# Tokens' rows that carry gate and token to the experts, and expert tiles that return finished tokens

## The chip, the cores and the metric

The kernel runs on 1 core of one Trainium2 chip. The metric is the device time of one execution in microseconds (us), lower is better. All data is float32.

## The reference

Four blocks, each with a residual, over x of 8 x 256 tokens of width 128. Each block normalises its input first.

```python
x = x + attn_a(layernorm(x))      # 16 heads, relative bias, full 256 x 256 scores
x = x + ffn(layernorm(x))
x = x + attn_b(layernorm(x))      # 16 heads, low-rank keys and values, causal in blocks of T = 256
x = x + ffn(layernorm(x))

def ffn(x, ...):                  # 8 experts, each token goes to one
    logits = xt @ Wr + br
    gates = max(softmax(logits))
    idx = argmax(logits)
    xn = layernorm(xt) * ln_g + ln_b
    h = relu(xn @ W1[idx] + b1[idx])      # 128 -> 512
    y = h @ W2[idx] + b2[idx]             # 512 -> 128
    return y * gates
```

The gate of a token is one over the sum of exp(logit - largest logit).

## The kernel before

The program runs two stages, `st` 0 and 1, each an attention and then an expert part. The 2,048 tokens are 16 tiles of 128; two tiles are one batch entry `b` of 0 to 7. Every engine's program is one list over the same steps `s`: steps 0 to 63 of a stage are the attention's units (a batch entry and two heads), and from step 65 on (`n = s - 65`) one expert tile each. The order within a step is written out by hand (`step`, `after`, `routes`), so an engine does its instructions of a step in that order and waits in place for what is not there.

**Routing.** After a batch entry's attention, `post_a` and `post_a2` normalise it, GpSimd multiplies and adds ln_g and ln_b, `post_c` forms the logits and `choose` the one-hot choice on VectorE. TensorE counts (`post_d`), ScalarE copies the counts, and `place` on VectorE turns them into a row number in `xs_scratch` for each token. Entries 1, 3, 5, 6 and 7 route 4, 4, 4, 2 and 2 tiles. GpSimd sends a tile with one indirect DMA (`send`, L303): 128 rows of 129 floats, the normalised token and its own number. `xs_scratch`, one for each stage, is filled first with rows whose number is out of bounds (`fill`, L1454, SyncE's queue, 9 DMAs a stage).

**Experts.** A stage has 25 tiles of 128 rows. `index` computes where each tile's rows lie and which expert it has (part 3, at n = 11, for the last five). SyncE gathers tiles into `f_xs`, which has 24 slots (L1465). `XT` (L419) transposes them on TensorE in groups of four, ScalarE copies them out (L898), `H` (L668) multiplies by W1, ScalarE's `relu` (L906) follows, `Y` (L682) multiplies by W2. On VectorE `W` (L1309) copies the next tile's W1, b1 and b2, and `Y` (L1316) adds b2 to the result into one of 8 slots of `f_ys`. GpSimd's `back` (L322) scatters the slot to the tokens' rows of `ys_scratch`; rows with a number out of bounds are left out. Step n does H of tile n, Y of tile n - 2 and W of tile n + 2. TensorE's Y of a tile waits for VectorE's Y of the tile two before, and `W` waits for the `Y` that frees its buffer.

**Gates.** `gates` (L1332 and L930) forms them for 12 and then 4 tiles at n = 15 and n = 17: two VectorE instructions, Exp on ScalarE, two on VectorE.

**Return.** SyncE (`results`, L1478) reads `ys_scratch` into `xn`, in five pieces. VectorE's `add` (L1087) forms x + gate * y, in stage 0 before the next norm (`pre_a`, then GpSimd's power L291 and `pre_a2`), in stage 1 before the write to the output: the last piece is read by ScalarE's queue (L1016), added, and sent out by it (L1018).

## Time and profile before

| what | us |
|---|---|
| median of 3 runs | 693.21 |
| lowest and highest run | 689.38 and 693.81 |
| the profiled execution | 694.63 |
| its span, first to last instruction | 693.4 |
| around its span | 1.2 |

TensorE is busy for 94% of the span. The chain of waits follows the work that ended last back to the start; the timeline lists instructions in order of time; a bracket behind a row tells how long its engine had stood idle and what ended that. Windows give busy time per engine in a stretch. A queue's name (SPq, ACTq) marks the issue of a DMA.

### The profile page before, as it was taken

The page shows a single profiled execution, that of the slowest core. Times are in us where ns is not written, and L with a number is a line of the kernel's source. Part 1 is how long each engine was busy: PE and PEld are TensorE (multiplying, and loading weights), DVE is VectorE, ACT ScalarE, POOL GpSimd, SP SyncE. Part 2 cuts the span into 40 slices and gives each one's busy share as a digit, 9 for nine tenths or more (in the row PEclk, how much of TensorE's full clock was granted, in tenths as well). Part 3 has the DMA queues.
Part 4 walks back from the last instruction along what each step waited for, and adds up shares of the span by engine and source line. Part 5 has one row for each costly group of instructions (what it writes and reads, how often), then busy time and mean ns, then how long its engine had stood idle before and what let it go on. Part 6 is the DMA issues. An engine that isn't in the chain of part 4 may idle for free.

```text
span 693.4 us, 17716 instructions
## 1 busy us (share of the span) xinstructions
PE 655.1 (94%) x5406; PEld 551.3 (80%) x5406; DVE 471.9 (68%) x2113; ACT 534.2 (77%) x1768; POOL 361.1 (52%) x672
## 2 busy tenths in 40 slices
PE   6899999999999999999898999999999999989894
PEld 5678787888888888779796787888788888868893
DVE  3876767676777767966354668687768668896433
ACT  3788888788888879765664989898989889874462
POOL 3344635465556555636462446465745655644552
PEclk9999999999999999999998999999999999999998
DMA  9999999920000000014220000000000000020214
GB/s 265 193 182 180 211 248 182 183 38 6 1 6 5 9 1 10 24 40 151 79 63 16 2 1 3 1 1 6 14 2 1 10 10 1 17 47 17 78 31 127
DMA packets 71212, 42.71 MB, mean 62 GB/s; under 512 B 7953, under 2 KB 68254, under 8 KB 70864
## 3 DMA queue, kind: packets, MB, share of 16 engines
q1 hardware_dynamic: 66336, 36.31, 27.5%
q0 software_dynamic: 2624, 4.23, 1.9%
q10 hardware_dynamic: 2160, 1.05, 0.6%
q8 instruction: 45, 0.74, 0.5%
q14 instruction: 47, 0.39, 0.2%
HBM read 17.68 MB, written 25.06 MB: 62 GB/s over the span
## 4 chain that ended last, share of the span: by engine, by line
PE 79%; DVE 10%; issue 4%; ACT 3%; DMA 1%; POOL 1%; SPq 0%; DVEq 0%; POOLq 0%; ACTq 0%
PE ps L419 15%; PE ps L565 13%; PE ps L528 13%; PE ps L414 9%; PE ps L416 8%; PE ps L415 8%; PE ps L668 6%; PE ps L682 5%; DVE ring L1151 3%; ACT ring L857 1%; PE ps L602 1%; DMA wkn<-in_w_qkv 1%; ACT f_ht L906 1%; PE ps L620 1%; POOL ys_scratch L322 1%
## 5 line engine op out<-in xcount | busy, mean ns | idle before, releaser
L315 POOL TENSOR_SCALAR ring<-ring,rs 128x256 f32<-128x256 f32 (+1 forms) x500 | 220.0, 458 | 219.7 <-DVE rs L1162 218.7
L857 ACT ACTIVATE ring<-ring,mn 128x256 f32<-128x256 f32 (+1 forms) x512 | 243.4, 488 | 0.0
L419 PE MATMUL ps<-ident,ring 128*128 128x128 f32 x896 | 121.8, 275 | 3.7 <-POOL ring L315 2.4
L528 PE MATMUL ps<-qk 64*128 64x256 f32 (+1 forms) x1024 | 115.0, 363 | 0.2 <-ACT qk L825 0.2
L565 PE MATMUL ps<-pt,v 128*64 128x256 f32 (+1 forms) x1024 | 111.9, 359 | 2.0 <-DVE pt L1178 1.3
L419 PEld LDWEIGHTS ps<-ident,ring 128*128 128x128 f32 x896 | 102.2, 142 | 11.1 <-POOL ring L315 3.5
L857 ACT ACTIVATION_READ_ACCUMULATOR ring<-ring,mn 128x1 f32 x512 | 104.1, 203 | 0.0
L565 PEld LDWEIGHTS ps<-pt,v 128*64 128x64 f32 x1024 | 65.8, 136 | 46.2 <-issue 13.1
L528 PEld LDWEIGHTS ps<-qk 64*128 64x128 f32 x1024 | 82.6, 187 | 18.3 <-issue 8.5
L825 ACT COPY qk<-ps 128x512 f32<-128x512 f32 x128 | 74.8, 585 | 28.4 <-PE ps L416 26.9
L1151 DVE CUSTOM_DVE_ANT_0 ring<-ps,cm 128x128 f32<-128x128 f32 (+1 forms) x256 | 73.6, 350 | 6.3 <-PE ps L528 6.2
L322 POOL DMA_INDIRECT ys_scratch<-f_ys,f_xs x50 | 51.1, 1023 | 39.3 <-DVE f_ys L1316 27.3
L1180 DVE COPY pt<-ps 128x512 f32<-128x512 f32 x64 | 44.1, 689 | 35.2 <-PE ps L419 35.1
L414 PE MATMUL ps<-xth,wqkh 128*128 128x256 f32 x192 | 65.9, 343 | 0.0
L906 ACT ACTIVATE f_ht<-ps,f_w 128x128 f32<-128x128 f32 x136 | 38.5, 371 | 31.3 <-PE ps L668 25.3
L682 PE MATMUL ps<-w,f_ht 128*128 (+1 forms) x400 | 53.1, 278 | 5.6 <-DVE f_ys L1316 4.7
L1151 DVE CUSTOM_DVE_ANT_0 ring<-ps,T 128x256 f32<-128x256 f32 x136 | 55.4, 417 | 0.0
L416 PE MATMUL ps<-xtl,wqkh 128*128 128x256 f32 x192 | 55.0, 286 | 0.0
L415 PE MATMUL ps<-xth,wqkl 128*128 128x256 f32 x192 | 54.7, 285 | 0.0
L779 ACT ACTIVATE oh<-ps 128x512 fp32r<-128x512 f32 x64 | 38.4, 600 | 20.8 <-PE ps L565 20.8
L682 PEld LDWEIGHTS ps<-w,f_ht 128*128 128x128 f32 x400 | 48.2, 192 | 7.5 <-issue 7.3
L414 PEld LDWEIGHTS ps<-xth,wqkh 128*128 128x128 f32 x192 | 36.9, 192 | 18.7 <-issue 17.5
(209 smaller groups left out, 1339.2 us busy)
## 6 DMA issues: line engine op xcount, KB each, us to landing
xs_scratch<-padt SPq DMA_DIRECT2D x16, 1032.0 KB, 18.5
w<-in_W SPq DMA_DIRECT2D x16, 256.0 KB, 5.4
f_xs<-xs_scratch SPq DMA_DIRECT2D x50, 64.5 KB, 2.0
xs_scratch<-padt SPq DMA_DIRECT2D x2, 838.5 KB, 16.7
T<-in_bias SPq DMA_DIRECT2D x2, 512.0 KB, 8.2
T<-in_bias SPq DMA_DIRECT2D x1, 1024.0 KB, 11.1
bu<-in_w_kv_up SPq DMA_DIRECT2D x1, 1024.0 KB, 7.9
ys_scratch<-f_ys,f_xs POOLq DMA_INDIRECT x50
```

The costliest lines, as they stand in the source:

```text
L315: i = pool.tensor_scalar(ring[:, hh, it, 0:w], ring[:, hh, it, 0:w], rs[:, q], 1.0, ALU.mult, ALU.mult)
L322: pool.indirect_dma_start(ys_dram[st], bass.IndirectOffsetOnAxis(ap=f_xs[:, n % NX, 128:129].bitcast(U32), axis=0), f_ys[:, n % NY, :], No ...
L414: pe.matmul(out, ah, bh, start=first, stop=False)
L415: pe.matmul(out, al, bh, start=False, stop=False)
L416: return pe.matmul(out, ah, bl, start=False, stop=last)
L419: return pe.transpose(out, src, ident[:, :])
L528: i = pe.matmul(PS[u % 2][hh][:, 256 * it:256 * it + w], qk[rows, 128 * it:128 * it + 128], qk[rows, 256:256 + w], start=True, stop=True)
L565: i = pe.matmul(PO[64 * hh:64 * hh + 64, col + lo:col + 256], a_v[b % 2][:, jt, 128 * c + 64 * hh:128 * c + 64 * hh + 64], a_pt[(U0 + u) % ...
L682: i = pe.matmul(y_bank(n)[:, 0:128], f_ht[n % 3][:, 128 * f:128 * f + 128], w2[:, bass.ds(e * 4 + f, 1), :].rearrange("p a n -> p (a n)"), ...
L825: act.copy(a_qk[(U0 + u) % 2][:, :], PT_[:, :]).then_inc(a_t, 1)
L857: i = act.activation(ring[:, hh, it, 0:w], ring[:, hh, it, 0:w], ACT.Exp, bias=mn[:, q], scale=-1.0, accum_out=sm[:, q])
L1151: i = dve.tensor_tensor_reduce(ring[:, hh, it, 0:w], bank[:, 256 * it:256 * it + w], table(st, 2 * c + hh, it), 1.0, BIG, ALU.add, ALU.min ...
```

## The change

A token's row becomes `ROW` = 258 floats: normalised token (0 to 127), its number (128), its gate (129) and the token itself (130 to 257). `xn`, `numbers`, `gate` and `x` become views of one tile `row`. The fill, the sends and the gathers move 1,032 bytes a row. The slots of `f_xs` go from 24 to 12. The gates are formed route by route: one subtraction in `choose`, Exp on ScalarE one step later, the sum and the reciprocal in `place`. VectorE's `Y` has a second instruction that multiplies by the gate and adds the token. The scatter of stage 1 writes the output tensor; that of stage 0 writes `ys_scratch`, which is read back into `x`. `add`, `finish`, the final output DMAs and `d_out` and `v_end` are gone.

```diff
-NX = 24
+NX = 12
+ROW = 258
-POST = {"a": 14, "b": 15, "c": 16, "lg": 16, "d": 18, "place": 18}
-GATES = (15, 17)
+POST = {"a": 14, "b": 15, "c": 16, "lg": 16, "gate": 17, "d": 18, "place": 18}
...
-    xs_dram = [nc.dram_tensor(f"xs_scratch{st}", (XROWS, 129), F32).ap() for st in range(2)]
-    ys_dram = [nc.dram_tensor(f"ys_scratch{st}", (NT * 128, 128), F32).ap() for st in range(2)]
-    x = sb("x", [128, NT, 128])
+    xs_dram = [nc.dram_tensor(f"xs_scratch{st}", (XROWS, ROW), F32).ap() for st in range(2)]
+    ys_dram = [nc.dram_tensor("ys_scratch", (NT * 128, 128), F32).ap(), t["out"].rearrange("b s d -> (b s) d")]
+    row = sb("row", [128, NT, ROW])
+    xn, numbers, gate, x = row[:, :, 0:128], row[:, :, 128:129], row[:, :, 129:130], row[:, :, 130:ROW]
...
-    f_xs = sb("f_xs", [128, NX, 129])
+    f_xs = sb("f_xs", [128, NX, ROW])
...
-                xs_dram[st], bass.IndirectOffsetOnAxis(ap=posi[:, j:j + 1].bitcast(U32), axis=0), xn[:, j, :], None
+                xs_dram[st], bass.IndirectOffsetOnAxis(ap=posi[:, j:j + 1].bitcast(U32), axis=0), row[:, j, :], None
...
-        def gates(c):
-            m = CH[c][1] - CH[c][0]
-            act.wait_ge(v_gs, 2 * st + c + 1)
+        def gates(b):
+            r = NR * st + ROUTE_NO[b]
+            m = ROUTED[b][1] - ROUTED[b][0]
+            act.wait_ge(v_gs, r + 1)
             act.activation(f_sub[:, 0:m, :], f_sub[:, 0:m, :], ACT.Exp).then_inc(a_ge, 1)
...
+            if (b := post_at(s, "gate")) is not None and b in ROUTED:
+                gates(b)
             if (b := post_at(s, "d")) is not None and b in ROUTED:
                 post_d(b)
...
-        j0, j1 = BACK[-1]
-        for i in range(NY):
-            act.wait_ge(d_ys[i], 2 * 16 * len(range(i, NF, NY)))
-        act.dma_start(xn[:, j0:j1, 0:128], ysv[1][:, j0:j1, :]).then_inc(d_yt[-1], 16)
-        act.wait_ge(v_end, len(BACK))
-        act.dma_start(ov[:, j0:j1, :], x[:, j0:j1, :]).then_inc(d_out, 16)
...
         V(dve.tensor_reduce(g, l, AX, ALU.max))
+        dve.tensor_tensor(f_sub[:, 0:n, :], l, by_tile(g, n), ALU.subtract).then_inc(v_gs, 1)
         V(dve.tensor_tensor(h, l, by_tile(g, n), ALU.is_ge))
...
         V(dve.tensor_copy(bas[:, 0, :], run[:, :]))
+        dve.wait_ge(a_ge, r + 1)
+        G = gate[:, t0:t1, :].rearrange("p t a -> p (t a)")
+        V(dve.tensor_reduce(G, f_sub[:, 0:n, :], AX, ALU.add))
+        V(dve.reciprocal(G, G))
         dve.wait_ge(a_cnt, r + 1)
...
-                add(0, 2 * b)
-                V(add(0, 2 * b + 1))
+                for j in range(2 * b, 2 * b + 2):
+                    dve.wait_ge(d_yt[BACK_OF[j]], 16)
...
-            dve.tensor_tensor(f_ys[:, n % NY, :], y_bank(n)[:, 0:128], first_layer(n)[:, 512:640], ALU.add
-                              ).then_inc(v_fy, 1)
+            V(dve.tensor_tensor(f_ys[:, n % NY, :], y_bank(n)[:, 0:128], first_layer(n)[:, 512:640], ALU.add))
+            dve.scalar_tensor_tensor(f_ys[:, n % NY, :], f_ys[:, n % NY, :], f_xs[:, n % NX, 129:130], f_xs[:, n % NX, 130:ROW],
+                                     ALU.mult, ALU.add).then_inc(v_fy, 1)
...
-                sp.dma_start(xn[:, j0:j1, 0:128], ysv[st][:, j0:j1, :]).then_inc(d_yt[g], 16)
+                sp.dma_start(x[:, j0:j1, :], ysv[:, j0:j1, :]).then_inc(d_yt[g], 16)
...
-        results(1, 0)
-        results(1, 1)
-        for g, (j0, j1) in enumerate(BACK[:-1]):
-            sp.wait_ge(v_end, g + 1)
-            sp.dma_start(ov[:, j0:j1, :], x[:, j0:j1, :]).then_inc(d_out, 16)
-        sp.wait_ge(d_out, 16 * len(BACK))
+        for i in range(NY):
+            sp.wait_ge(d_ys[i], 2 * 16 * len(range(i, NF, NY)))
```

A gather of tile n of 12 or more waits, by the code that was there, until the scatter of tile n - NX has landed; with 24 slots only tile 24 did.

## Rows read from the trace of the kernel before

**Rows 1.** The page: busy time, share of the span and instructions of each engine

```profile
PE 655.1 (94%) x5406; PEld 551.3 (80%) x5406; DVE 471.9 (68%) x2113; ACT 534.2 (77%) x1768; POOL 361.1 (52%) x672
```

**Rows 2.** Chain of waits in order of time, its end: start, us, what

```profile
684.65 2.29 DMA ys_scratch<-f_ys,f_xs
686.94 0.02 issue
686.96 2.60 DMA xn<-ys_scratch
689.56 0.02 issue
689.58 1.14 DVE x L1087 x4
```

**Rows 3.** Timeline of the last 11 us: start, us, engine, line, idle before

```profile
683.59 0.29 DVE L1316 TENSOR_TENSOR f_ys<-ps,f_w 128x128 f32<-128x128 f32 x1 [1.30 <-PE ps L682]
683.79 3.23 DVE L1087 SCALAR_TENSOR_TENSOR x<-xn,gate,x 128x128 f32<-128x128 f32 x12
...
690.75 0.38 ACTq L1018 DMA_DIRECT2D out<-x  x1
```

**Rows 4.** Who waited for `f_ys`, us and times, over the whole span

```profile
  PE ps L682: 4.7, 4
  DVE f_w L1309: 1.7, 7
```

**Rows 5.** Windows: us; busy us (instructions) of PE, PEld, DVE, ACT, POOL; PEclk, DMA share, GB/s

```profile
78.00:92.00 14.00, 14.00 (x114) 11.42 (x112) 9.54 (x41) 12.33 (x38) 7.02 (x15) 1.00 1.10 351
...
95.00:130.00 35.00, 35.00 (x285) 28.85 (x282) 25.80 (x113) 29.17 (x91) 16.88 (x35) 1.00 1.27 182
...
150.00:180.00 30.00, 30.00 (x242) 24.58 (x239) 20.64 (x89) 24.30 (x73) 16.93 (x33) 1.00 0.02 6
```

**Rows 6.** Timeline, VectorE, stage 0, the last batch entry beside tiles 1 to 4

```profile
313.58 0.28 DVE L1188 TENSOR_TENSOR x<-ps,x 128x128 f32<-128x128 f32 x1
313.90 0.29 DVE L1189 TENSOR_TENSOR x<-ps,x 128x128 f32<-128x128 f32 x1
...
323.57 0.17 DVE L1073 TENSOR_TENSOR bas<-cnt,bas 128x8 f32<-128x8 f32 x1 [0.86 <-ACT cnt L880]
```

**Rows 7.** Instructions of `gate`: durations min/median/max in ns

```profile
L1087 DVE SCALAR_TENSOR_TENSOR x<-xn,gate,x x32: 321/346/465, 361.3 to 690.4; 128x128 f32<-128x128 f32 x32
```

**Rows 8.** Timeline, all engines, stage 1, tiles 8 to 11

```profile
653.23 0.29 DVE L1316 TENSOR_TENSOR f_ys<-ps,f_w 128x128 f32<-128x128 f32 x1 [3.67 <-PE ps L682]
653.32 1.14 ACT L906 ACTIVATE f_ht<-ps,f_w 128x128 f32<-128x128 f32 x4 [2.62 <-remote]
...
653.78 1.15 PE L682 MATMUL ps<-w,f_ht 128*128 x8 [1.61 <-DVE f_ys L1316]
...
656.22 1.15 PE L682 MATMUL ps<-w,f_ht 128*128 x8 [0.85 <-DVE f_ys L1316]
```

**Rows 9.** Waits, TensorE, 605 to 686 us: us in total, times, longest

```profile
PE ps L419 <- DMA f_xs<-xs_scratch: 0.4, 1, 0.4
...
PE ps L668 <- DVE f_w L1309: 0.3, 1, 0.3
```

**Rows 10.** Timeline around the hand-over to stage 1

```profile
361.33 0.61 DVE L1087 SCALAR_TENSOR_TENSOR x<-xn,gate,x 128x128 f32<-128x128 f32 x2
...
362.58 0.98 POOL L322 DMA_INDIRECT ys_scratch<-f_ys,f_xs  x1 [0.30 <-issue]
...
363.57 0.75 POOL L291 TENSOR_TENSOR rstd<-rstd,half 128x2 f32<-128x2 f32 x1
...
367.44 0.41 PE L414 MATMUL ps<-xth,wqkh 128*128 128x256 f32 x1
...
375.60 0.28 PE L414 MATMUL ps<-lth,wqkh 128*128 128x256 f32 x1
```

**Rows 11.** Timeline, SyncE's queue: the fills of both stages, the first gathers

```profile
21.07 42.30 SPq L1454 DMA_DIRECT2D xs_scratch<-padt  x9
...
86.88 46.56 SPq L1454 DMA_DIRECT2D xs_scratch<-padt  x9
291.25 8.71 SPq L1465 DMA_DIRECT2D f_xs<-xs_scratch  x12
```

**Rows 12.** Windows, columns as in rows 5: where the fill of stage 0 ends

```profile
72.00:74.00 2.00, 2.00 (x17) 1.83 (x17) 1.62 (x7) 1.74 (x4) 1.74 (x4) 1.00 0.72 94
74.00:76.00 2.00, 2.00 (x20) 1.79 (x20) 1.40 (x4) 2.00 (x8) 1.08 (x3) 1.00 0.37 15
```

**Rows 13.** Instructions of `xs_scratch`: ns min/median/max, first and last start in us

```profile
L303 POOL DMA_INDIRECT xs_scratch<-xn,posi x32: 957/1102/1261, 134.6 to 647.5; - x32
```

**Rows 14.** DMA issues: count, KB each, median us from issue to landing

```profile
f_xs<-xs_scratch SPq DMA_DIRECT2D x50, 64.5 KB, 2.0
```

**Rows 15.** Timeline, stage 1: scatter of tile 11, and the transposes of tiles 20 to 23

```profile
659.30 0.98 POOL L322 DMA_INDIRECT ys_scratch<-f_ys,f_xs  x1 [0.30 <-issue]
...
668.97 0.60 PE L419 MATMUL ps<-ident,f_xs 128*128 128x128 f32 x4
```

**Rows 16.** Windows, columns as in rows 5: the hand-over, and stage 1's tiles 8 to 17

```profile
366.00:376.00 10.00, 8.85 (x44) 7.03 (x45) 2.26 (x14) 2.73 (x5) 0.97 (x1) 0.66 0.10 28
...
650.00:672.00 22.00, 19.20 (x168) 18.59 (x167) 7.02 (x31) 13.04 (x44) 10.79 (x11) 1.00 0.25 69
```

More of the change, by code:

```diff
@@ L68 @@
 PRE_0 = {"a": -4, "a2": -3, "b": -2, "c": -1}
[L70 to L72 removed]
+LAST_POST = {"sums": 68, "a": 69, "b": 70, "c": 70, "lg": 71, "gate": 71, "d": 71, "place": 72}
+POST = {"a": 14, "b": 15, "c": 16, "lg": 16, "gate": 17, "d": 18, "place": 18}
 INDEX = {60: 0, 62: 1, 65: 2, 76: 3}
@@ L987, in step @@
                 next_weights(n)
-            if n in GATES:
-                gates(GATES.index(n))
         def after(s):
@@ L1083, in start_rows @@
         V(dve.tensor_copy(run[:, :], rows_e[:, 0:NE]))
-    def add(st, j):
-        dve.wait_ge(d_yt[BACK_OF[j]], 16 * (st + 1))
-        return dve.scalar_tensor_tensor(x[:, j, :], xn[:, j, 0:128], gate[:, j:j + 1], x[:, j, :], ALU.mult, ALU.add)
     def table(st, h, it):
@@ L1416, in step @@
                 next_weights(n)
-            if n in GATES:
-                gates(GATES.index(n))
-            if st and NF + 1 <= n < NF + 3:
-                for j in ((0, 1, 2, 3), range(4, 12))[n - NF - 1]:
-                    finish(j)
         def routes(s):
@@ L1445, in dve_program @@
                 steps[1](s - OFF)
-        for j in range(*CH[1]):
-            finish(j)
     def fill(st):
```

47 lines of the change are left out of this document (15 added, 32 removed).

## The prediction, made before the result was known

> **What bounds the kernel now.** I read the page first: TensorE is busy for 94% of the span, VectorE for 68%, ScalarE for 77%, GpSimd for 52% [rows 1]. So what counts is what TensorE waits for, and what stands behind its last matmul. Then the end of the chain of waits: the last scatter lands at 686.94, is read back for 2.60 us, four additions take 1.14 us, and the output DMA is issued at 690.75 [rows 2, 3]. The reader is to see that from 683.88 to 693.4 no matmul runs, and that all after 686.94 is the return of tokens. Then the waits for `f_ys` and the timeline of the expert parts, for where VectorE holds TensorE up: TensorE waits on it 4 times in both stages, and the weight copy 7 times [rows 4]. Last the windows, for what the fill costs: 285 matmuls in 35 us beside it and 242 in 30 us without it, 8.1 a us in both, TensorE busy throughout [rows 5]. The fill costs the attention nothing.
>
> **The end.** Removed is all between the last landing, 686.94, and the end of the span, 693.40, but for the 0.04 us in which a queue sees it (the chain shows 0.02 at each such step [rows 2]): 6.42 us. The scatter goes to the output with the same 512 bytes a row; nothing shows a write to another tensor to cost otherwise, so it lands as before. Also gone are 12 additions that lay beside the scatters [rows 3], worth nothing here.
>
> **VectorE's Y.** It now has a dependent second instruction. A dependent pair starts 0.32 us apart (313.58 and 313.90 [rows 6]); the removed addition has the very form of the new instruction and takes 0.346 us [rows 7]. A tile is thus done 0.32 + 0.346 = 0.67 us after its start where it was 0.29 [rows 3]: +0.38 us. 50 of them are 19 us of VectorE's time, nearly all beside matmuls. Where it is not hidden:
> - The last tile: the scatter behind it starts 0.38 later. +0.38.
> - Tiles 8 and 9 of each stage. TensorE's Y of tile 10 waited 1.61 us for VectorE's Y of tile 8; then the 11 small instructions of `index` part 3, then Y of tile 9, for which TensorE's Y of tile 11 waited 0.85 us [rows 8]. Both are in one chain: 2 x 0.38 = 0.76.
> - Seven weight copies waited for a Y [rows 4], and TensorE's H waited once for such a copy in stage 1 [rows 9]; I take one a stage: 0.38. But ScalarE stood 2.62 us and VectorE 3.67 us just before tile 8's Y, and the trace doesn't name the cause of the first ("remote") [rows 8]; a standstill of another cause would swallow what came before it. So 0.76 to 1.14 a stage; I take 1.0, for two stages +2.0. The bounds: 0, if other waits end last, and (4 + 7) x 0.38 = 4.2 for both stages, if each wait seen is lengthened in full.
>
> **The hand-over to stage 1.** Two additions before the norm go, 0.61 us [rows 10]. But the norm's power (L291) stands on GpSimd behind the scatter of tile 22, which ran until 363.56; the power started at once [rows 10]. That scatter waits for VectorE's Y, so it comes 0.38 later and the 0.61 is won where nobody waits. +0.38, between -0.3 and +0.4. In the attention of stage 1 fourteen more additions go, from an engine that has slack there: nothing.
>
> **The gates.** Route by route: three instructions of VectorE of about 0.17 us (the small ones of `place` [rows 6]) and a short Exp, five times a stage. The two in `place` stand before the wait for the counts. For the last entry that wait was 0.86 us [rows 6], which covers both; the one in `choose` delays the count by 0.1 to 0.2 us, and TensorE transposes a group before it counts. Behind `place` stand the W and Y of the next tiles, and GpSimd's two sends. In the attention VectorE is busy for 20.64 of 30 us and ScalarE for 24.30 [rows 5], and both orders leave a step between Exp and its reader. Cost 0, at most 0.2 a route. The eight old instructions at tiles 13 and 15 go; no TensorE wait stands there. 0.
>
> **The rows of 1,032 bytes.** The fill: its 9 DMAs are issued from 21.07 on [rows 11], and the traffic falls to 94 and then 15 GB/s between 72 and 76 [rows 12], so it ends near 75: 54 us. The bytes double. If each byte costs what it costs now, at 182 GB/s, it ends at 21 + 108 = 129; at the 351 GB/s at which the weights load in other pieces, at 75 [rows 5]. The first send, which waits for it, is at 134.6 [rows 13]. So it is hidden, with 5 us to spare at worst. The second fill, whose issue starts 23.5 us behind the end of the first's [rows 11], would at the lower rate end near 129 + 23 + 108 = 260; the first gathers stand behind it on SyncE's queue at 291 [rows 11].
> The sends: 1.10 us on GpSimd each [rows 13], for 128 rows. If that counts rows, nothing changes; if a wide row counts as two, each doubles. I take the first, since the row count alone stays.
> The gathers: 64.5 KB land in 2.0 us [rows 14]; the added 64.5 KB are 0.18 us at 351 GB/s and 0.35 at 182. TensorE waited 0.4 us for the first group in stage 1 [rows 9], so a delay there counts. I take 0.3 a stage, +0.6, between 0 and 4 x 0.35 x 2 = 2.8.
> The Trainium skill, DMA: Bandwidth & Descriptors, Anatomy of one DMA, has a DMA cost about 2 us fixed plus its bytes at 436 GB/s. By it the added half is 0.15 us and the term 0.3 instead of 0.6; the trace's 2.0 us for 64.5 KB agrees.
>
> **Twelve slots.** A gather of tile 23 now waits for the scatter of tile 11, which starts at 659.30 and, at 2.29 us like the last one [rows 2], lands at 661.6; the gather lands 2.0 later, at 663.6, while its transposes are at 668.97 [rows 15]. 5 us of cover; behind it on SyncE's queue stand only tile 24's gather and the read-back. The groups before have scatters long done. 0.
>
> **The sum**, against the profiled execution's span: -6.42 + 0.38 + 2.0 + 0.38 + 0.6 = -3.06, from 693.4 to 690.3 (691.6 with the 1.2 around it). The profiled execution is 1.4 above the median of the runs; the same difference from the median, 693.21, gives 690.2.
>
> **The rivals.**
> - *All the VectorE work is hidden.* For it: only 4 waits of TensorE on `f_ys` [rows 4], and a standstill of unnamed cause before the two I charge. Against: both waits stand with their lengths. -6.42 + 0.38 + 0.38 = -5.7: 687.5.
> - *It is hidden and the clock stays up.* The clock falls at the hand-over: the mean is 0.66 of full in the 10 us from 366 [rows 16], so 6.8 us at 1.2 GHz after TensorE had stood for parts of the 2 us before; a 128x256 matmul takes 0.41 us there and 0.28 at 2.4 GHz [rows 10]. If it didn't fall, 6.8 x (1 - 0.28 / 0.41) = 2.2 more are won: 685.3. Little speaks for it, the gap gets no shorter by my sum.
> - *The clock falls in the expert parts.* They run at 1.00 now [rows 16] with waits of 1.61 and 0.85 us close together [rows 8], which get longer. One such fall costs 2.2, as above, two stages 4.4: -3.06 + 4.4 = +1.3: 694.5. The Trainium skill, TensorE: Matmul & The Clock Gate, The HAM clock gate, says that idleness halves the clock; the trace agrees at the hand-over and does not show it at the waits of tiles 10 and 11.
> - *Wide rows count double on GpSimd.* Then the two last sends before tile 12's gather come 2 x 1.1 = 2.2 us later a stage, and TensorE waits for that group: 4.4, again 694.5. For it: nothing in the trace, whose rows of 512 and 516 bytes are too alike.
> - *The fill blocks the first send* (the slower side). GpSimd waits at L303 for the whole fill, and behind it stands the scaling of the softmax (L315), on which TensorE's transposes wait. It decides when the fill takes over 134.6 - 21.1 = 113.5 us, 2.1 times now for twice the bytes; each us beyond is a us of the kernel, and from 123.5 us (2.3 times) on the kernel is over 1% slower than before. At three times, 162 us: +48.5 - 3.1 = 45 slower, 739. For it: only 5 us to spare, and the present rate is half of that of the weights, so bytes aren't all that a fill costs. Against: the pieces get larger, and for the byte price to rise they would have to run worse than the small ones.
>
> **How the numbers follow.** About 1% (7 us) is what a measurement of this kernel can tell from no change. Chances: my forecast 0.50, hidden 0.17, hidden with the clock 0.08, clock falls 0.08, sends double 0.10, fill blocks 0.07. The likeliest gives 690.2. The range, 686.5 to 695.5, takes in the forecast, the hidden case, the clock's fall and the doubled sends, 0.85 together; the upper bounds of Y (+2.2) and of the gathers (+2.2) together lead to 694.6. Faster by over 1% needs under 686.3: the case with the clock, and little for the spread of runs, 0.10. Slower needs over 700.1: the fill in most of its cases, and two of the others together, 0.07. Within 1%: 0.83.
>
> **What would show it.** Right: the span ends within 0.1 us of the last scatter's landing; VectorE's Y pair takes 0.67 us; the waits of TensorE's Y of tiles 10 and 11 grow by about 0.4 each; the first send still starts near 134.6; the hand-over's power starts right behind a scatter. Wrong: sends over 1.5 us on GpSimd, a gather of tiles 12 to 23 ahead of its transposes by nothing, a granted clock under 1.00 between 630 and 670, or attention steps that got longer.

## The result, and the profile after

| what | before, us | after, us |
|---|---|---|
| median of 7 runs each | 692.03 | 686.75 |
| lowest and highest run | 689.38 and 693.81 | 685.44 and 688.04 |
| profiled execution | 694.63 | 687.1 |
| its span | 693.4 | 685.9 |

The ratio after to before is 0.992, 95% interval 0.990 to 0.9941: 5.3 us less, 0.8%. That is inside "within 1%", and inside the forecast range by only 0.25 us (its lower end is 686.5). But 3.1 us less was forecast, so the size has to be explained.

The page of after first, busy time by engine:

```profile
PE 652.9 (95%) x5406; PEld 549.8 (80%) x5406; DVE 482.1 (70%) x2145; ACT 533.3 (78%) x1774; POOL 358.8 (52%) x672
```

VectorE is busy 10.2 us longer than in [rows 1], TensorE 2.2 us less, with the same 5,406 matmuls. Where the time went is seen when each execution is cut at the same instructions: the start of ScalarE's copy of a unit's queries and keys (attention), of the first `relu` of a tile (expert part), and of the last scatter. These starts are read off the traces. The 48 units are units 8 to 55 of the 64 of an attention, in every run.

| stretch, us | before | after | difference |
|---|---|---|---|
| 48 units of stage 0's attention | 213.17 | 213.17 | 0.00 |
| stage 0, relu of tile 0 to tile 12 | 38.12 | 39.30 | +1.18 |
| stage 0, tile 12 to tile 24 | 24.12 | 23.57 | -0.55 |
| tile 24 to stage 1's first unit | 7.77 | 8.15 | +0.38 |
| 48 units of stage 1's attention | 188.21 | 186.29 | -1.92 |
| stage 1, tile 0 to tile 12 | 37.14 | 38.41 | +1.27 |
| stage 1, tile 12 to tile 24 | 22.80 | 23.00 | +0.20 |
| last relu to last scatter | 3.55 | 3.95 | +0.40 |
| last scatter to the end of the span | 8.74 | 2.11 | -6.63 |

The spans differ by 7.5 us. 1.6 of that lie ahead of unit 8 of stage 0; there the two profiles of before (before and before_again) differ by 2.1 from each other, so the change need have no part in it. The rest, 0.3, lies in the stretches between those of the table. The second profiles of both kernels, on other chips, give before 23.36 for stage 0's tiles 12 to 24 (so the -0.55 is spread), and the same 188.15 and 186.30 for stage 1's attention. For tile 24 to stage 1's first unit they give 7.37 and 7.63: this stretch differs by 0.4 to 0.5 between profiles of one kernel, and its 0.38 is read from one wait below instead.

**The end.** The timeline of after (start, length in us, engine, line, output<-input; in brackets the idle time before and what ended it):

```profile
682.29 0.29 DVE L1313 TENSOR_TENSOR f_ys<-ps,f_w 128x128 f32<-128x128 f32 x1 [0.91 <-PE ps L682]
682.61 0.35 DVE L1314 SCALAR_TENSOR_TENSOR f_ys<-f_ys,f_xs 128x128 f32<-128x128 f32 x1
683.76 0.98 POOL L322 DMA_INDIRECT out<-f_ys,f_xs  x1 [0.61 <-issue]
```

The reader is to see the pair of VectorE, whose second starts 0.32 us behind the first and takes 0.35, and that nothing follows the last scatter: it starts at 683.76 and the span ends at 685.9. In [rows 2, 3] a read of 2.60, four additions and an output DMA followed the same scatter.

**The weight copies.** Waits of TensorE in after, from 310 to 330 us (stage 0) and from 627 to 641 us (stage 1); us in total, times, longest:

```profile
PE ps L668 <- DVE f_w L1306: 0.7, 1, 0.7
PE ps L620 <- ACT pT L872: 0.5, 1, 0.5
```

Both windows give these two lines. Before, the first was 0.3 in both stages (for stage 1 see [rows 9]). It is H of tile 5, and VectorE in after shows why (timeline, stage 1):

```profile
633.15 0.28 DVE L1313 TENSOR_TENSOR f_ys<-ps,f_w 128x128 f32<-128x128 f32 x1
633.47 0.35 DVE L1314 SCALAR_TENSOR_TENSOR f_ys<-f_ys,f_xs 128x128 f32<-128x128 f32 x1
633.97 0.50 DVE L1306 COPY f_w<-w 128x644 f32 x1
```

```profile
634.52 1.16 PE L668 MATMUL ps<-f_xt,f_w 128*128 128x128 f32 x8 [0.67 <-DVE f_w L1306]
```

The new instruction stands ahead of the copy, which starts 0.82 us behind the start of Y (0.42 in before), and TensorE's H starts when the copy ends. Its wait is 0.67 and 0.67 us in the two stages of after, 0.28 and 0.28 in before, and the same to 0.01 in the second profiles. Relu of tile 4 to tile 5 is 2.33 us before and 2.72 after in both stages.

**Tiles 8 to 11.** Timeline of after, stage 1:

```profile
650.85 2.17 ACT L906 ACTIVATE f_ht<-ps,f_w 128x128 f32<-128x128 f32 x8 [3.29 <-PE ps L668]
650.95 0.29 DVE L1313 TENSOR_TENSOR f_ys<-ps,f_w 128x128 f32<-128x128 f32 x1 [1.69 <-remote]
...
652.14 1.15 PE L682 MATMUL ps<-w,f_ht 128*128 x8 [0.79 <-ACT f_ht L906]
...
654.72 1.15 PE L682 MATMUL ps<-w,f_ht 128*128 x8 [0.65 <-DVE f_ys L1314]
```

Where [rows 8] has waits of 1.61 and 0.85 for VectorE, after has 0.79 for ScalarE and 0.65 for VectorE. These two did not grow. But after has a third one just ahead, at H of tile 11, where before has none:

```profile
648.76 0.50 DVE L1306 COPY f_w<-w 128x644 f32 x1
649.31 1.16 PE L668 MATMUL ps<-f_xt,f_w 128*128 128x128 f32 x8 [1.09 <-issue]
```

The row names nobody who ended it; H starts 0.05 us behind the end of the weight copy. The three waits of tiles 10 and 11 make 2.53 us in stage 1 (2.46 in before) and 2.76 in stage 0 (2.25 in before). Beside them ScalarE and GpSimd stand still as well, as in before, and no cause is named for it ("remote").

**The hand-over.** Timeline of after:

```profile
360.91 0.29 DVE L1033 BATCH_NORM_STATS2 stats<-row 128x6 f32<-128x128 f32 x1
...
362.16 0.98 POOL L322 DMA_INDIRECT ys_scratch<-f_ys,f_xs  x1 [0.30 <-issue]
...
363.15 0.74 POOL L291 TENSOR_TENSOR rstd<-rstd,half 128x2 f32<-128x2 f32 x1
363.93 0.66 DVE L1044 TENSOR_SCALAR xh<-row,mv,rstd 128x128 f32<-128x128 f32 x2 [1.08 <-POOL rstd L291]
```

The power starts 0.01 us behind the scatter, as in [rows 10]; VectorE had its part ready at 361.88, 1.3 us earlier. TensorE's wait for the output of this norm, first in before and then in after:

```profile
365.16 0.41 PE L419 MATMUL ps<-ident,xh 128*128 128x128 f32 x2 [0.70 <-DVE xh L1049]
```

```profile
364.74 0.41 PE L419 MATMUL ps<-ident,xh 128*128 128x128 f32 x2 [1.08 <-DVE xh L1044]
```

It is 0.70 and 1.08 in the second profiles too: +0.38.

**The fill and the sends.** One window of after beside the second fill (columns as in [rows 5]), and the instructions of `xs_scratch` on GpSimd (ns min/median/max, first and last start):

```profile
95.00:130.00 35.00, 35.00 (x286) 28.61 (x286) 25.83 (x113) 29.52 (x93) 17.74 (x36) 1.00 1.10 314
```

```profile
L303 POOL DMA_INDIRECT xs_scratch<-row,posi x32: 959/1078/1253, 133.4 to 644.9; - x32
```

The same 35 us moved 182 GB/s at a DMA share of 1.27 before [rows 5] and 314 GB/s at 1.10 after. The sends take what they took [rows 13], and the first starts at 133.4. TensorE ran 286 matmuls beside it (285 before).

### The profile page after: what moved, and what is told of

It reads as the page before. It is cut to its first block, busy times and chain, and to the rows that moved or that the text cites. A ratio compares the mean times of both kernels' runs of the same rounds, so it can differ in the third digit from the quotient of the medians.

```text
span 685.9 us, 17753 instructions
## 1 busy us (share of the span) xinstructions
PE 652.9 (95%) x5406; PEld 549.8 (80%) x5406; DVE 482.1 (70%) x2145; ACT 533.3 (78%) x1774; POOL 358.8 (52%) x672
## 4 chain that ended last, share of the span: by engine, by line
PE 82%; DVE 9%; issue 3%; ACT 2%; POOL 1%; DMA 1%; another core or an unknown queue 1%; SPq 0%; DVEq 0%; POOLq 0%; ACTq 0%
PE ps L419 16%; PE ps L565 14%; PE ps L528 14%; PE ps L414 10%; PE ps L416 8%; PE ps L415 8%; PE ps L668 5%; PE ps L682 4%; DVE ring L1148 2%; DMA wvn<-in_w_qkv 1%; PE ps L602 1%; PE ps L620 1%; ACT f_ht L906 1%; DVE f_ys L1314 1%
## 5 line engine op out<-in xcount | busy, mean ns | idle before, releaser
L419 PE MATMUL ps<-ident,ring 128*128 128x128 f32 x896 | 120.4, 274 | 2.5 <-POOL ring L315 2.4
L419 PEld LDWEIGHTS ps<-ident,ring 128*128 128x128 f32 x896 | 102.4, 142 | 8.2 <-POOL ring L315 3.5
L1148 DVE CUSTOM_DVE_ANT_0 ring<-ps,T 128x256 f32<-128x256 f32 x136 | 55.5, 417 | 0.0
L1148 DVE CUSTOM_DVE_ANT_1 ring<-ps,T 128x256 f32<-128x256 f32 x120 | 50.0, 417 | 0.0
```

What stands on the lines that cost most here:

```text
L419: return pe.transpose(out, src, ident[:, :])
L1148: i = dve.tensor_tensor_reduce(ring[:, hh, it, 0:w], bank[:, 256 * it:256 * it + w], table(st, 2 * c + hh, it), 1.0, BIG, ALU.add, ALU.min ...
```

## The experiments

Names that begin with a are edits of after, with b edits of before. They ran in four series, each on another chip, with before in each. Ratios are to before, with their 95% interval; behind stand the median of the edit and that of before in its series. Four questions: what the end is worth and why; whether Y costs what was charged; which edit gives the 1.9 us in stage 1's attention; what wide rows and gates cost.

### The end

**a_tail_back**: after, but stage 1's scatters go to a second scratch tensor, and the tokens are read back and written out by two DMAs each way on SyncE, without additions.

```diff
-    ys_dram = [nc.dram_tensor("ys_scratch", (NT * 128, 128), F32).ap(), t["out"].rearrange("b s d -> (b s) d")]
+    ys_dram = [nc.dram_tensor(f"ys_scratch{st}", (NT * 128, 128), F32).ap() for st in range(2)]
...
+        sp.dma_start(x[:, j0:j1, :], ysv1[:, j0:j1, :]).then_inc(d_yt[-1], 16)
+        sp.dma_start(x[:, 0:j0, :], ysv1[:, 0:j0, :]).then_inc(d_yt[0], 16)
+        sp.wait_ge(d_yt[-1], 32)
+        sp.dma_start(ov[:, j0:j1, :], x[:, j0:j1, :]).then_inc(d_yt[-1], 16)
```

> The changed kernel with the end of the old one but for its additions: stage 1 scatters to a scratch tensor, which is read back and then written to the output. Theory: the end costs two more DMAs, 2.60 us and 2.6 us as before, so it is 5.2 us slower than the changed one, about 692, ratio 1.000, and the missing 1.2 of the removed 6.4 us were the additions. Rival: what the change won at the end is more than those parts (the wait for the scatter itself is shorter when it goes to the output), so that it stays at 690 or below, ratio 0.997 or less.

Measured: 1.0089 [1.0062, 1.0116], 696.81 against 690.82, where 1.000 was expected. From the last scatter to the end it is 12.88 us. The experiment was too coarse: all tiles go home behind the last scatter, where before has only the last pieces there. a_tail_staged has before's pieces.

**a_tail_staged**: the same, but three pieces are read behind the scatters that complete them, and the last by ScalarE's queue, as in before.

```diff
+        act.dma_start(x[:, j0:j1, :], ysv1[:, j0:j1, :]).then_inc(d_yt[-1], 16)
+        act.wait_ge(d_yt[-1], 32)
+        act.dma_start(ov[:, j0:j1, :], x[:, j0:j1, :]).then_inc(d_out, 16)
```

> The changed kernel with the old end but for its additions, read back in pieces while the last tiles still run, and the last piece on ScalarE's queue. Theory: 11.7 us of the run with the whole read-back at the end were the unstaged 0.9 MB; staged, what remains over the changed kernel is the last piece's read-back and the output DMA, 2.6 + 2.6 = 5.2 us, ratio to before 0.9995. Rival: reading straight after the scatter is dearer than the profile of before shows, 7 us or more, ratio over 1.002.

Measured: 1.0041 [1.0025, 1.0058], 689.46 against 686.59, and after_again in the same series 0.9925: 7.6 us between the two medians, where 5.2 was expected. Its timeline, the end:

```profile
680.77 0.98 POOL L325 DMA_INDIRECT ys_scratch<-f_ys,f_xs  x1 [0.61 <-issue]
682.93 0.36 SPq L1519 DMA_DIRECT2D row<-ys_scratch  x1
682.93 0.46 ACTq L1020 DMA_DIRECT2D row<-ys_scratch  x1
683.34 2.58 SPq L1522 DMA_DIRECT2D out<-row  x4
685.86 0.38 ACTq L1022 DMA_DIRECT2D out<-row  x1
```

From 680.77 to the end of the span at 689.3 it is 8.58 us, against 2.11 in after: 6.47, with no addition there. The read takes 2.9 us from issue to issue (2.6 in before), the output 3.5 (2.6), now beside SyncE's four; that these four are why it takes longer was not tested. So before's end was 2.60 us of read, 1.14 of additions and 2.6 of output. That 6.47 comes out here without additions, close to before's sum, is chance.

### Y of VectorE

**a_y_single**: after without the new instruction, so that it leaves out gate and token.

```diff
-            V(dve.tensor_tensor(f_ys[:, n % NY, :], y_bank(n)[:, 0:128], first_layer(n)[:, 512:640], ALU.add))
-            dve.scalar_tensor_tensor(f_ys[:, n % NY, :], f_ys[:, n % NY, :], f_xs[:, n % NX, 129:130], f_xs[:, n % NX, 130:ROW],
-                                     ALU.mult, ALU.add).then_inc(v_fy, 1)
+            dve.tensor_tensor(f_ys[:, n % NY, :], y_bank(n)[:, 0:128], first_layer(n)[:, 512:640], ALU.add).then_inc(v_fy, 1)
```

> The changed kernel without the second instruction of VectorE's Y: the experts' results go back without gate and without the token, so this part of the computation is left out. Theory: the two expert parts and the hand-over lost 1.2 us (stage 0) and 1.6 us (stage 1) by the 0.38 us a tile on the chain over tiles 8 to 11 and at the last tile; without it they run as before, and the kernel is 2.5 to 3 us faster than the changed one, about 684, ratio 0.988. Rival: the loss there comes from the wide rows, whose gathers land 0.4 us later (2.4 us for 2.0); then it is under 1 us faster, 686, ratio 0.991.

Measured: 0.9903 [0.9869, 0.9937], 685.52 against 690.82. By the ratios that is 1.2 us faster than after (0.992 [0.990, 0.9941]), with intervals that overlap, where 2.5 to 3 was expected; the runs don't tell this from the rival's under 1 us. In its profile last relu to last scatter is 3.56 (3.95 with it), relu 4 to relu 5 again 2.33, the hand-over 6.98 (8.15). Its tiles 0 to 12 of stage 0 say nothing: the granted clock fell there, to a mean of 0.88 in the 14 us from 324.

**b_y_double**: before with a second instruction of that form in Y, which adds the tile's normalised row, and the same again, **b_y_double2**, on another chip.

```diff
+            V(dve.tensor_tensor(f_ys[:, n % NY, :], y_bank(n)[:, 0:128], first_layer(n)[:, 512:640], ALU.add))
+            dve.scalar_tensor_tensor(f_ys[:, n % NY, :], f_ys[:, n % NY, :], ones[:, 0:1], f_xs[:, n % NX, 0:128],
+                                     ALU.mult, ALU.add).then_inc(v_fy, 1)
```

> The kernel before with a second, dependent instruction in VectorE's Y, of the form that the changed kernel has (result * 1 + the tile's row of 128 floats, so that part of the result is another). Theory: 0.38 us more behind each product cost the two expert parts 0.8 to 1.2 us each, the hand-over and the end 0.4 each: 2.4 to 3 us slower than before, ratio 1.004. Rival: the products' wait is elsewhere and all of it but the last tile is hidden: 0.4 us, ratio 1.001.

> The kernel before with a second, dependent instruction in VectorE's Y. Theory: it delays the last route's choice and placing as well as the products, so tile 12's gather comes 0.4 to 0.5 us later where that is what TensorE waits for: 0.8 to 1.2 us a stage with or without the standstill, ratio 1.004. Rival: without the standstill it is hidden in the expert parts, and only the hand-over and the end, 0.4 each, remain: 1.001.

Measured: 1.004 [1.0025, 1.0056], 695.42 against 692.34, and 1.0062 [1.0038, 1.0086], 696.1 against 692.37: 2.8 and 4.3 us. Tiles 0 to 12 take 40.28 and 40.12 in stage 0 (38.12 and 38.11 before), 38.37 and 39.03 in stage 1 (37.14 and 37.29); in b_y_double2 the clock fell in both stretches, so only 40.28 and 38.37 can be compared: +2.2 and +1.2. The first loss is at tile 5 in both stages, 0.4 us, the wait for `f_w` seen above. The other is at tiles 9 to 11. In stage 0 of b_y_double the two waits of tiles 10 and 11 are 2.00 and 1.27, against 1.65 and 0.60 in before (1.63 and 0.88 in before_again): there they grew about as the prediction had it. In its stage 1 they are 0.84 and 0.98, with 1.04 at H of tile 11 between them, the picture of after. The forecast's terms for all of Y, 2.0 + 0.38 + 0.38, make 2.8.

**a_u_early**: after, but b2 + ... is turned round: U forms b2 * gate + token one step before the product is there, and Y is one instruction behind the product.

```diff
+            dve.scalar_tensor_tensor(f_ys[:, n % NY, :], first_layer(n)[:, 512:640], f_xs[:, n % NX, 129:130],
+                                     f_xs[:, n % NX, 130:ROW], ALU.mult, ALU.add).then_inc(v_u, 1)
...
+            dve.scalar_tensor_tensor(f_ys[:, n % NY, :], y_bank(n)[:, 0:128], f_xs[:, n % NX, 129:130], f_ys[:, n % NY, :],
```

> The changed kernel with VectorE's Y in another order: b2 * gate + token is formed one step before the product is there, and when it is, one instruction (product * gate + that) ends the tile. VectorE has as many instructions, but only one behind TensorE. Theory: what the expert parts lost is the 0.38 us that the second instruction adds behind the product; with it gone (0.35 for 0.67 us) the kernel is 1 to 2.5 us faster than the changed one, 684.3 to 685.7, ratio 0.989 to 0.990. Rival: it is VectorE's total time that counts, which stays; then no change from 686.8, 0.992.

Measured: 0.9918 [0.989, 0.9946], 685.22 against 690.82. That is the ratio of after, as the rival had it: the runs show no gain. In the profile last relu to last scatter is 3.63, tiles 0 to 12 38.60 and 37.88, and the wait for `f_w` at tile 5 0.34: shorter than in after by 0.3 to 0.7 each. VectorE does as many instructions as in after, so in these stretches part of Y's price is that the pair stands between the product and the scatter, and not its work. But the attention of stage 1 takes 186.75, 0.46 more than in after, and why wasn't looked into.

**a_u_pow**: a_u_early, and the hand-over's power stands on GpSimd ahead of the scatter that delayed it.

```diff
+            if st == 0 and s == OFF + PRE_0["a"]:
+                pool_pow(rstd, half[:, 0:2], v_var0, p_pow0, NB + 1)
             if 0 <= n - 2 < NF:
                 back(n - 2)
```

> The changed kernel with one instruction of VectorE behind the product (b2 * gate + token formed a step ahead), and with the power of stage 1's first norm ahead of the scatter of tile 22 on GpSimd. Theory: the first part gives 0.5 to 0.7 us in each expert part and 0.3 at the end, as the profile of the kernel with it alone shows (38.60 and 37.88 us for tiles 0 to 12); the second lets the power start when its input is there, 1 us earlier, of which TensorE, which has tile 24's Y to do first, can use 0.5. Together 2 us faster than the changed kernel in this call, ratio to before 0.989. Rival: the total of VectorE's and GpSimd's time decides, or spare time elsewhere takes both: ratio 0.992.

Measured: 0.9908 [0.9888, 0.9929], 680.37 against 686.59; after_again in this series 681.86. Of the versions that compute everything it has the lowest ratio, 1.5 us under after_again, though the two intervals overlap. Its hand-over, the timeline:

```profile
359.62 0.72 POOL L291 TENSOR_TENSOR rstd<-rstd,half 128x2 f32<-128x2 f32 x1 [0.37 <-DVE rstd L1042]
...
360.38 0.60 DVE L1046 TENSOR_SCALAR xh<-row,mv,rstd 128x128 f32<-128x128 f32 x2
360.54 1.09 POOL L322 DMA_INDIRECT ys_scratch<-f_ys,f_xs  x1 [0.20 <-issue]
```

From relu 24 to stage 1's first unit it takes 6.10 us (after_again 7.63), and the eight units behind it 24.67 (25.78). The clock did not fall there either, so the two differences hold the power's new place and the clock's, and no run separates them. The next windows are of a_u_pow and then of after:

```profile
358.00:378.00 20.00, 17.13 (x121) 13.03 (x119) 10.98 (x59) 12.07 (x39) 8.50 (x14) 1.00 0.15 42
```

```profile
358.00:378.00 20.00, 16.85 (x107) 13.70 (x105) 8.79 (x41) 8.13 (x24) 6.43 (x7) 0.83 0.19 54
```

The same 20 us hold 121 matmuls at a mean of 1.00 and 107 at 0.83 (partly at 1.2 GHz). The two windows do not begin at the same instruction, so only the clock is to be read from them.

### The additions ahead of stage 1's norms

**a_adds_back**: after with two instructions of the additions' form again ahead of each norm of stage 1.

```diff
+                    i = dve.scalar_tensor_tensor(x[:, j, :], x[:, j, :], 0.0, x[:, j, :], ALU.mult, ALU.add)
+                V(i)
```

> The changed kernel, with two additions a batch entry put back ahead of stage 1's norms (x * 0 + x, of the same form and size as the ones removed; every value stays). Theory: the two additions stood ahead of VectorE's copies for which TensorE's transposes waited (1.2 us in 3 waits in stage 1's attention before, none after), so they are what the attention of stage 1 gave back: about 2.1 us between its first and last unit. Then this kernel is 2.1 us slower than the changed one, about 688.9 us, ratio to before about 0.995, and the units of stage 1 take as long as before. Rival: the gain there comes from the gates' new places or from the read-back that lands in x; then the additions cost nothing as I predicted, and it stays at 686.8, 0.992.

Measured: 0.9962 [0.9945, 0.9979], 688.3 against 690.82. By the ratios that is 2.9 us slower than after, and the two intervals don't overlap. The attention of stage 1 takes 187.53 in its profile (after 186.29): +1.24, less than the 2.1 expected.

**b_no_adds**: before without these sixteen additions, so that it leaves out what the experts of stage 0 give, and nothing else changed.

```diff
-                add(0, 2 * b)
-                V(add(0, 2 * b + 1))
+                for j in range(2 * b, 2 * b + 2):
+                    dve.wait_ge(d_yt[BACK_OF[j]], 16)
```

> The kernel before without the 16 additions ahead of stage 1's norms: what the experts of stage 0 give is left out of x. Theory: the additions cost the attention of stage 1 about 2.1 us, so this is 2 to 2.5 us faster than before (ratio 0.997), and the gain grows step by step along stage 1's units. Rival: no difference, 1.000, as I predicted for them; at the hand-over the power of the norm stands behind a scatter in any case.

Measured: 0.9964 [0.995, 0.9977], 690.08 against 692.34. The attention of stage 1 takes 185.54 (before 188.21): 2.7 us. TensorE's waits in it, 376 to 595 us, of before and then of b_no_adds:

```profile
PE ps L419 <- DVE pt L1178: 1.2, 3, 0.5
PE ps L419 <- POOL ring L315: 0.4, 1, 0.4
PE ps L414 <- DVE mn L1151: 0.4, 1, 0.4
```

```profile
PE ps L419 <- POOL ring L315: 0.4, 1, 0.4
PE ps L414 <- DVE mn L1151: 0.4, 1, 0.4
```

The wait for `pt` is gone. But it is 1.2 us, and 2.7 are gone. The rest is seen when the two traces are laid side by side matmul by matmul (both have the same 5,406 in the same order) and it is noted where before falls further behind. It does so at one place in each of the six batch entries of the 48 units, at the transposes of L419 behind the additions:

| start in before, us | 405.41 | 436.55 | 467.98 | 499.52 | 530.94 | 562.43 | sum |
|---|---|---|---|---|---|---|---|
| falls behind b_no_adds by, us | 0.69 | 0.29 | 0.21 | 0.57 | 0.20 | 0.57 | 2.53 |

The list of waits has only the three of 0.57 and more, as idle time of 0.47, 0.35 and 0.35; ahead of the others TensorE stood for 0.07 us or less. What stands ahead of the first is seen on VectorE in before, and on TensorE behind it:

```profile
402.36 0.70 DVE L1087 SCALAR_TENSOR_TENSOR x<-xn,gate,x 128x128 f32<-128x128 f32 x2
403.10 0.29 DVE L1038 BATCH_NORM_STATS2 stats<-x 128x6 f32<-128x128 f32 x1
...
404.15 0.68 DVE L1033 TENSOR_TENSOR ol<-ps,oh 128x512 fp32r<-128x512 f32 x1
404.75 0.41 DVE L1177 COPY pt<-ps 128x256 f32<-128x256 f32 x1
405.08 0.28 DVE L1178 COPY pt<-ps 128x128 f32<-128x128 f32 x1
```

```profile
405.41 0.55 PE L419 MATMUL ps<-ident,ring 128*128 128x128 f32 x3 [0.47 <-DVE pt L1178]
```

In that step VectorE works without a gap from the additions through the norm and two copies out of PSUM, and TensorE's next transposes start when the last of them ends. The average slack of VectorE (68% busy) is not the slack of this step.

**b_adds_even**: before, with the additions of a batch entry one step earlier, an even step that has no norm in it.

```diff
-PRE = {"a": -7, "a2": -5, "b": -4, "c": -3}
+PRE = {"add": -8, "a": -7, "a2": -5, "b": -4, "c": -3}
...
+            if st and (b := pre_at(s, "add", st)):
+                adds(b)
```

> The kernel before with stage 1's additions (but the first two) one step earlier, at the end of an even step instead of ahead of the norm at the end of an odd one. The same instructions. Theory: the additions cost 2.7 us in 48 units because they lie ahead of the copy of transposed scores that frees a PSUM bank for TensorE; in an even step VectorE has time, and the 48 units take 185.5 to 186.5 us instead of 188.2, ratio 0.997. Rival: VectorE's total time or its share of the memory counts: 188.2 us, ratio 1.000.

Measured: 0.9981 [0.9967, 0.9995], 685.46 against 686.59. The attention of stage 1 takes 186.73, 1.5 of the 2.7 us, and no wait for `pt` is left in it. So more than half was the place and not the work. The other 1.2 us are the same fault in the new step. TensorE's waits from 376 to 595 us have a line that neither before nor b_no_adds has, and VectorE shows what it is:

```profile
PE ps L528 <- DVE lg L1222: 0.8, 5, 0.2
```

```profile
422.04 0.60 DVE L1087 SCALAR_TENSOR_TENSOR x<-xn,gate,x 128x128 f32<-128x128 f32 x2
422.68 0.17 DVE L1222 TENSOR_TENSOR lg<-ps,brb 128x16 f32<-128x16 f32 x1
```

The moved additions stand ahead of the logits (`lg`), which VectorE takes out of PSUM, and five times TensorE's next matmul falls 0.23 us behind b_no_adds for it: 1.2 us.

### Wide rows, and gates

**b_wide** and **b_wide2**: before with rows of 258 floats in the fill, the sends and the gathers, and 12 slots; the added half is not used.

```diff
-NX = 24
+NX = 12
+ROW = 258
...
-    f_xs = sb("f_xs", [128, NX, 129])
+    f_xs = sb("f_xs", [128, NX, ROW])
```

> The kernel before with rows of 258 floats: fills, sends and gathers move 1,032 bytes a row, x lies in the rows' tile, and f_xs has 12 slots; gates, Y and the return are as before. Theory: the fill is hidden and the gathers land 0.4 us later, of which the expert parts show 0 to 0.6 us in all: ratio 1.000 to 1.001. Rival: the wide rows are what the expert parts lost: 2 us or more, ratio 1.003. As recorded for the changed kernel the fill runs at about 300 GB/s, so the first send does not wait in either case.

> The kernel before with rows of 1,032 bytes and 12 slots. Theory: without the standstill TensorE waits for tile 12's gather, and sends and gathers of twice the bytes come 0.2 + 0.4 us later, so tiles 0 to 12 take 0.4 to 0.6 us longer than with narrow rows; with the standstill, nothing, as found. Rival: nothing in either case.

Measured: 1.000 [0.9987, 1.0013], 692.23 against 692.34, and 0.9986 [0.9972, 1.0001], 691.18 against 692.37. Free, though TensorE's waits for the first gathers of the stages grew, from 0.49 and 0.44 in before to 0.81 and 0.83 in b_wide. The instructions of `xs_scratch` in b_wide:

```profile
L304 POOL DMA_INDIRECT xs_scratch<-row,posi x32: 956/1103/1257, 132.8 to 644.7; - x32
```

**b_gates** and **b_gates2**: before with the gates formed route by route.

```diff
+        dve.tensor_tensor(f_sub[:, 0:n, :], l, by_tile(g, n), ALU.subtract).then_inc(v_gs, 1)
...
+        dve.wait_ge(a_ge, r + 1)
+        G = gate[:, t0:t1]
+        V(dve.tensor_reduce(G, f_sub[:, 0:n, :], AX, ALU.add))
+        V(dve.reciprocal(G, G))
```

> The kernel before with the gates formed route by route, as in the changed kernel, and not at tiles 15 and 17. Theory: no cost in the attentions (an Exp and three small VectorE instructions a route, each with a step to spare) and none in the expert parts: 1.000. Rival: it frees VectorE where it was busy in stage 0's tiles 13 to 17 and is worth 0.5 to 1 us there, 0.999, or it costs VectorE and ScalarE up to 0.2 us a route in the attention, 1.002.

> The kernel before with the gates formed route by route. Theory: 0.6 us in stage 1's attention, as its profile showed before, and up to 0.4 us in each stage's tiles 0 to 12, since the last route's rows are placed later and tile 12's gather with them; ratio 1.001 to 1.002. Rival: its 1.0017 was chance, 1.000.

Measured: 1.0017 [1.0003, 1.0031], 693.62 against 692.34, and 1.0025 [1.0007, 1.0043], 694.08 against 692.37: 1.2 to 1.7 us. Laid beside before matmul by matmul, both fall behind by 0.32 to 0.37 us at two places of stage 1's attention that have nothing to do with the additions (at those of the additions they gain or lose up to 0.3, which profiles of before's own attention do too). In after, laid beside b_no_adds, the same two places cost 0.39 each. TensorE's waits in b_gates, 376 to 595 us, name it, and VectorE shows the new pair in the step ahead of the first:

```profile
PE ps L413 <- DVE ol L1033: 0.3, 2, 0.2
```

```profile
465.35 0.18 DVE L1074 TENSOR_REDUCE gate<-f_sub 128x4 f32<-128x32 f32 x1
465.57 0.18 DVE L1075 RECIPROCAL gate<-gate 128x4 f32<-128x4 f32 x1
...
470.69 0.65 DVE L1033 TENSOR_TENSOR ol<-ps,oh 128x512 fp32r<-128x512 f32 x1
```

From the pair in `place` to `ol`, for which TensorE waits, VectorE has no gap. These are the steps in which entries 1 and 3 are placed. A further 0.3 us lies between unit 56 of stage 0 and the relu of tile 0, beside the last routes (41.73 in both profiles, 41.44 and 41.42 in before's two). In stage 1 the first transposes of gathered rows waited 1.26 and 1.78 us (0.44 and 0.37 in before), but a_tail_back, which has the same gates as after, has 2.23 there where after has 0.60; so how much of that is the gates' isn't shown.

### The two kernels once more

> The changed kernel again, beside the next three on the same chip: the measure for them. Both theories expect the ratio to before found first, 0.992, and in the profile the same parts: 186.3 us for 48 units of stage 1's attention, 39.3 and 38.4 us for the tiles 0 to 12 of the two expert parts.

> The kernel before again, as the measure for the next three on the same chip. Ratio 1.000. Both theories: tiles 0 to 12 of the expert parts take 38.1 and 37.1 us if the standstill is there, and about 35.6 and 36 us (as with the additions moved) if not.

Measured: after 0.9925 [0.9907, 0.9944], 681.86 against 686.59; before 1.000 [0.9986, 1.0014], 691.91 against 692.37. The attention is as expected, but after_again's tiles 0 to 12 take 37.38 and 36.75, not 39.3 and 38.4. It is from the chip of a_u_pow, where TensorE has no wait at tiles 9 to 11 in any of the four profiles; the profiles from the other chips all have waits of 0.5 us or more there, but for stage 0 of a_y_single. There TensorE waits for the gathers instead. Waits of TensorE in stage 1, 603 to 684 us, of after_again and then of b_adds_even, on that chip:

```profile
PE ps L419 <- DMA f_xs<-xs_scratch: 2.7, 2, 1.8
```

```profile
PE ps L419 <- DMA f_xs<-xs_scratch: 1.0, 1, 1.0
```

In stage 0 it is 2.3 against 1.1. Nevertheless the ratio of after to before is the same there, 0.9925 and 0.992.

## Why the prediction was right or wrong

- **The end: right.** Forecast -6.42, measured -6.63 (8.74 to 2.11). The span ends 2.11 us after the last scatter's start, where its landing took 2.29 in before. a_tail_staged shows that with two trips through DRAM put back the end is 6.47 longer again.
- **The last tile: right.** +0.38 forecast, +0.40 measured.
- **Y in the expert parts: size about right, place half right.** +1.0 a stage forecast; +1.18 and +1.27 measured over tiles 0 to 12 of after, which hold the gates and the gathers too. The weight copy is as charged, 0.3 to 0.7 in both stages. The two waits of tiles 10 and 11 that were to grow by 0.4 each did not (0.79 and 0.65 in after, stage 1); a third one came, at H of tile 11, and the three together grew by 0.07 in stage 1 and 0.5 in stage 0. How the waits beside the standstill divide isn't explained. What the whole of Y costs in the runs depends on the direction: put into before it costs 2.8 to 4.3 us (b_y_double), at or above the 2.8 that its terms make; taken out of after it gives back 1.2 by the ratios, not clear of noise (a_y_single).
- **The hand-over: right.** +0.38 forecast; TensorE's wait for the norm grew by 0.38 in both pairs of profiles (0.70 to 1.08), by the cause that was named: the power starts right behind the scatter. In a_u_pow, where it stands ahead of it, the stretch is 1.5 us shorter, with the clock's part in it.
- **The additions in stage 1's attention: this step failed.** "Fourteen more additions go, from an engine that has slack there: nothing." They cost 2.7 us in the profile (b_no_adds; 2.3 in the medians, 2.5 by the ratio). After has the whole of it, for at the six places it runs as b_no_adds does, and gives 0.8 back where the gates stand: 1.9. The prediction names no row for the slack; all that it shows of VectorE's is the whole span [rows 1] and a window of 30 us of stage 0's attention [rows 5], where there are no additions. Before's waits for `pt`, 1.2 us in three, were to be seen in the trace. In their place the runs show that each pair of additions moved the copies out of PSUM behind it, and TensorE's transposes with them, by 0.2 to 0.7 us. Other profiles of kernels with before's attention fall behind b_no_adds by less, the least 1.75 (b_y_double2, 187.29), so the 2.7 has a spread of its own.
- **The gates: a small miss.** 0 forecast, 1.2 to 1.7 measured. The last entry was read in its own rows [rows 6], but the instructions in the attention were taken as covered by slack over 30 us [rows 5], which is the same fault: two of its steps in stage 1 cost 0.32 to 0.39 each. Attention steps that got longer were among the prediction's own signs of being wrong.
- **The rows of 1,032 bytes: right on the fill and the sends.** The cover was larger than charged, since wide rows are cheaper by the byte (314 against 182 GB/s). The attention of stage 0 takes 213.17 to 213.23 in all kernels that ran. A doubled gather lands in 2.4 us for 2.0: 0.4 more, where 0.18 to 0.35 was reckoned. The Trainium skill, DMA: Bandwidth & Descriptors, Anatomy of one DMA, gives the figure behind the prediction's 0.15 for DMAs issued from GpSimd; these are issued from SyncE, and the measured 0.4 decides. The gathers were charged 0.6; TensorE's waits for them grew by 0.9 in the profiles of before and after (0.5 and 0.4 to 1.2 and 0.6), by 2.9 on the other chip (1.1 and 1.0 to 2.3 and 2.7), and b_wide shows no loss in its runs. So a wait that grew did not cost its length; what paces the part behind it instead isn't shown.
- **Twelve slots: right.** SyncE issues the gathers of tiles 12 to 23 over 12.0 us where it took 8.9, and no transposes of tiles 16 to 24 wait for them.
- **The rivals.** *All VectorE work hidden* gives nearly the measured time, 687.5, and that is luck: Y's second instruction lengthens TensorE's waits, and the additions and the gates make up the difference. *The clock stays up* and *falls in the expert parts*: the hand-over's mean over the ten us from 366 is 0.68 in after (0.66 in [rows 16]), and the expert parts are at 1.00 in the profile of after (after_again has 0.98 in the 10 us from 670); in edits of both kernels it falls there, as the last section shows. *Sends double*, *the fill blocks*: excluded by b_wide.

The sum of the parts, each measured by itself: -6.6 at the end, +0.4 for the last tile, about +2.4 for Y in the expert parts and the hand-over (the lower 2.8 of b_y_double less the 0.4), -2.5 for the additions in the runs, +1.2 to +1.7 for the gates, 0 for wide rows. That is -5.1 to -4.6, against -5.3 measured; with the 4.3 of b_y_double2 in place of the 2.8 it would be 1.5 less. The forecast was 2.2 us short; the additions alone are 2.5 and the gates take 1.2 back. Of the remaining 0.9 the gathers, charged 0.6 and free in b_wide, and 0.2 at the end make 0.8. That the parts add up so well is chance in part, since each is known to 1 or 2 us only.

**What stays open.** Why additions put back into after (a_adds_back) cost only 1.24 us in the attention of its profile, when in before they cost 1.75 to 2.7. Where the rest of the gates' 1.2 to 1.7 us lies. What stops the engines at tiles 8 to 11 on three of the chips, and why TensorE's waits beside it divide differently from profile to profile.

## What to carry to other kernels

The busy share of an engine over a long window does not tell what one more, or one less, instruction costs. It is the step in which the instruction stands that tells: if the engine goes from it without a gap to a PSUM copy that TensorE waits for, the instruction is on the path. So for each instruction that a change adds or removes, read the timeline from it to the next thing that another engine waits for. Moved to another step it can meet the same fault there, as b_adds_even shows. A list of waits leaves out the short ones, here three of six; two traces with the same matmuls in the same order, laid side by side, show them all. A trip through DRAM and back at the very end, 6.4 us here with its additions, is worth a good deal of work ahead of it, since nothing hides it.

## What the runs showed of the hardware

- **A fill with wide rows ran faster by the byte.** 516 bytes a row: 182 GB/s at a DMA share of 1.27; 1,032: 314 GB/s at 1.10, over the same 35 us. By rows this is 353 and 304 a us, and divided by the share 278 and 277: in the engines' busy time a row cost the same at either size. The Trainium skill, DMA: Bandwidth & Descriptors, Why small descriptors are slow (HBM only), says that each piece carries a fixed overhead besides its bytes; the direction agrees, but the overhead that it gives (about 3 cycles and 32 bytes a piece) makes, as an estimate, about a tenth between these two sizes, and not the factor of 1.7 measured.
- **An indirect send on GpSimd does not cost more for wider rows.** 128 rows: 1.10 us at 516 bytes and 1.08 to 1.10 at 1,032. The number of rows was not varied.
- **A scatter straight into the output tensor took no longer than one into scratch**: 2.11 us from the last scatter's start to the end of the span in after; in a_tail_staged, into scratch, 2.16 to the read that waits for it; 2.29 to the landing in before [rows 2].
- **The granted clock falls at places that vary between executions of one kernel.** b_y_double and b_y_double2 are the same kernel. The same 20 us at the start of stage 1's expert part have a mean of 1.00 in the profile of the first and 0.83 in that of the second:

```profile
605.00:625.00 20.00, 16.93 (x147) 13.21 (x144) 18.47 (x88) 15.57 (x61) 10.06 (x21) 1.00 0.17 41
```

```profile
605.00:625.00 20.00, 18.06 (x134) 14.78 (x131) 17.12 (x78) 14.16 (x55) 8.70 (x18) 0.83 0.17 41
```

A stretch of one profile that holds such a fall can't be compared with one that doesn't; the runs' medians can.
